# Layer 0 attention with one head in each 32-row group of TensorE, and three elementwise passes of every tile on GpSimd

## The reference

```python
x = x + _L0_xattn_ref(_layernorm(x), ctx_2048, ...)
# in it: mask = normalised x, n = 16, e = 64, t = 256, H = 8 heads of d = 8
x = jnp.transpose(mask, (0, 2, 1))
qkv = x @ w_in.T + b_in
scores = jnp.einsum('bqhd,bkhd->bhqk', q, k) / jnp.sqrt(d)
scores = jnp.where(abs(i - j) <= 64, scores, neg)
attn = jax.nn.softmax(scores, axis=-1)
o = jnp.einsum('bhqk,bkhd->bqhd', attn, v).reshape(n, t, e) @ w_out.T + b_out
y = jax.nn.relu(jnp.transpose(o, (0, 2, 1))) * encodings      # the gate product
out = jnp.einsum('nit,io->not', y, w_ct) + b_ct[None, :, None]
```

## Time and profile before

| | us |
|---|---|
| median of 3 runs (361.88 to 362.2) | 361.92 |
| the profiled execution: its own time | 362.1 |
| its span | 360.4 |
| PE busy | 320.2 |
| DVE busy | 256.2 |
| ACT busy | 208.1 |
| GpSimd busy | 192.7 |

### The profile page before, as it was taken

How to read it: one execution, slowest core, us unless ns; L and a number is a source line. 1 busy time by engine, 2 the same in 40 slices (tenths; PEclk the granted TensorE clock), 3 DMA queues, 4 the chain that set the end, 5 groups by cost and what they waited for, 6 DMA issues and landing times.

```text
span 360.4 us, 7398 instructions
## 1 busy us (share of the span) xinstructions
PE 320.2 (89%) x2258; PEld 252.3 (70%) x2258; DVE 256.2 (71%) x935; ACT 208.1 (58%) x438; POOL 192.7 (53%) x287
## 2 busy tenths in 40 slices
PE   0689999779798898999999999899999999999993
PEld 0467768567576666767777777777777767888892
DVE  5899999999989899988323615576478846661364
ACT  2639888759687695967841341467577865213210
POOL 4757988758767585856602431515152543244733
PEclk9859999999999999999999999999999999999997
DMA  7996000000000000000000000000000000000011
GB/s 220 363 373 227 1 3 3 1 2 3 1 2 0 3 3 1 3 2 2 2 2 0 0 2 0 1 2 0 2 3 0 2 0 3 0 31 15 1 38 37
DMA packets 10150, 12.16 MB, mean 34 GB/s; under 512 B 1920, under 2 KB 8832, under 8 KB 10112
## 3 DMA queue, kind: packets, MB, share of 16 engines
q1 hardware_dynamic: 9536, 11.36, 9.2%
q10 hardware_dynamic: 576, 0.33, 0.4%
HBM read 10.64 MB, written 1.05 MB: 32 GB/s over the span
## 4 chain that ended last, share of the span: by engine, by line
PE 58%; DVE 27%; issue 8%; ACT 3%; POOL 2%; DMA 1%; POOLq 0%; DVEq 0%; SPq 0%; ACTq 0%
DVE masked L1110 10%; PE S L666 6%; PE S L339 5%; PE O L377 4%; PE ST L690 4%; PE S L472 4%; PE ST L361 4%; PE S L608 2%; PE S L536 2%; PE PJ L449 2%; PE PJ L579 2%; PE O L623 2%; PE PJ L310 2%; DVE st L1072 2%; PE XB L597 2%
## 5 line engine op out<-in xcount | busy, mean ns | idle before, releaser
L1110 DVE CUSTOM_DVE_ANT_0 masked<-S,band 128x192 bf16<-128x192 f32 x256 | 79.1, 353 | 8.4 <-PE S L339 7.3
L785 ACT ACTIVATE ex<-ST 128x384 f32<-128x384 f32 x128 | 62.2, 489 | 14.0 <-PE ST L361 13.4
L339 PE MATMUL S<-qk 128*128 128x384 f32 x128 | 53.5, 424 | 10.2 <-DVE mw L1110 8.1
L948 POOL TENSOR_SCALAR rstd<-mv 128x1 f32<-128x1 f32 x40 | 11.8, 294 | 94.2 <-DVE mv L1074 94.0
L960 POOL TENSOR_TENSOR qk<-kp,kmask 128x1024 fp32r<-128x1024 f32 x24 | 46.3, 1934 | 5.0 <-DVE kp L1208 4.9
L361 PE MATMUL ST<-qk 128*128 128x192 f32 x256 | 48.7, 273 | 0.0
L361 PEld LDWEIGHTS ST<-qk 128*128 128x128 f32 x256 | 44.5, 189 | 1.9 <-issue 1.2
L339 PEld LDWEIGHTS S<-qk 128*128 128x128 f32 x128 | 24.8, 195 | 23.3 <-issue 16.1
L1254 DVE TENSOR_REDUCE mw<-S 128x8 f32<-128x512 f32 x32 | 22.0, 687 | 17.9 <-PE S L536 17.8
L751 ACT ACTIVATE hs<-PJ,sb,cols 128x512 fp32r<-128x512 f32 x29 | 22.5, 777 | 20.6 <-PE PJ L311 20.1
L377 PE MATMUL O<-ex,v 128*32 128x192 f32 x512 | 34.2, 338 | 0.0
(11 more groups left out here) (178 smaller groups left out, 757.9 us busy)
## 6 DMA issues: line engine op xcount, KB each, us to landing
w<-in_w SPq DMA_DIRECT2D x2, 1024.0 KB, 10.1
cx<-in_cx SPq DMA_DIRECT2D x1, 1024.0 KB, 7.9
cxT<-in_cxT SPq DMA_DIRECT2D x1, 1024.0 KB, 9.6
up<-in_up SPq DMA_DIRECT2D x1, 1024.0 KB, 10.9
down<-in_down SPq DMA_DIRECT2D x1, 1024.0 KB, 11.8
out<-x SPq DMA_DIRECT2D x8, 128.0 KB, 1.7
x<-in_x SPq DMA_DIRECT2D x1, 768.0 KB, 5.6
vecs<-in_vecs SPq DMA_DIRECT2D x1, 640.0 KB, 8.0
```

Of the source, the lines that this page charges most:

```text
L339: mm(out, r32(qp[:, t % 2, g, b, P * c:P * c + P]), r32(mv_), start=True, stop=True).then_inc(s["pe_s"], 1)
L785: A(ex[:, (n // 2) % 4, 2 * w:2 * w + 2, :], ST[n % 2][:, 0:2 * WIN].rearrange("p (h k) -> p h k", h=2), ACT.Exp, scale=SCALE).then_inc(s[ ...
L1110: last = V.tensor_tensor_reduce(out=masked[:, n % 2, h, :], in0=S[n % 2][:, WIN * h:WIN * h + WIN], in1=band[:, c, :], scale=1.0, scalar=N ...
```

## The change

A head of a group now has its own 32 rows (`rows(j)`), in the order given by a permuted `w0` (`w0p`, copied by GpSimd), `b0` and `colp`. A unit is one head with both query halves. A score product has 32 rows and 192 columns: two for the scores and two for the transposed scores, all four in one row group; before it was one of 128 rows by 384 columns and two of 128 rows by 192. The masked keys `kb` and all that builds them (GpSimd L960, ACT L761) are gone. The negated maxima come from a GpSimd scale of 128x16 (`neg`), and PE adds them to the queries in `MT` (one product of 512 columns and four of 128) in place of four transposes; ACT copies 128 rows of `MT` instead of 32.

The gate product and both normalisations move from DVE to GpSimd (except tile 0's `xn`). `ST_LAG` goes from 11 to 13, and what follows it moves by one or two slots. GpSimd does the selects of four units in a row instead of two. Loads on the ACT queue grow from 4 to 11: `b0` in four parts and `colp` in four. `mw` and the memset of it move behind the units.

```diff
-ST_LAG, PV_LAG = 11, 16
+NEG_LAG, MT_LAG, ST_LAG, PV_LAG, O_LAG = 9, 10, 13, (16, 18), 26
@@ PE, slot_
-                    mv_ = kb[:, t % 2, g, 2 * w:2 * w + 2, b, BAND * c:BAND * c + WIN]
-                    out = S[n % 2][:, 0:2 * WIN].rearrange("p (h k) -> p h k", h=2)
-                    mm(out, r32(qp[:, t % 2, g, b, P * c:P * c + P]), r32(mv_), start=True, stop=True).then_inc(s["pe_s"], 1)
+                    for c in range(2):
+                        last = mm(S[n % 2][:, WIN * c:WIN * c + WIN], r32(qp[rows(j), t % 2, g, b, P * c:P * c + P]),
+                                  r32(kp[rows(j), t % 3, g, b, BAND * c:BAND * c + WIN]), start=True, stop=True)
+                    last.then_inc(s["pe_s"], 1)
-                    for h in range(2):
-                        last = mm(ST[n % 2][:, WIN * h:WIN * h + WIN], r32(kb[:, t % 2, g, 2 * w + h, b, P * c:P * c + P]),
-                                  r32(qp[:, t % 2, g, b, BAND * c:BAND * c + WIN]), start=True, stop=True)
+                    for c in range(2):
+                        last = mm(ST[n % 2][:, WIN * c:WIN * c + WIN], r32(kp[rows(j), t % 3, g, b, P * c:P * c + P]),
+                                  r32(qm[rows(j), t % 2, g, b, BAND * c:BAND * c + WIN]), start=True, stop=True)
+                    pe.wait_ge(s["pool_neg"], k + 1)
+                    mm(MT[:, :].rearrange("p (g q) -> p g q", g=2), r32(identr[:, :]), r32(qp[:, t % 2, :, b, :]), start=True, stop=False)
+                            last = mm(MT[:, T * g + P * c:T * g + P * c + P], r32(neg[:, b, 2 * c + g, :]), r32(identr[:, :]),
+                                      start=False, stop=(g, c) == (1, 1))
@@ ACT
-            load(b0[:, :], a["b0"], "ld_w0")
+            for j in range(4):
+                load(b0[rows(j), :], a["b0"].rearrange("(r j d) n -> j r d n", r=4, j=4)[j], "ld_b0")
+                load(colp[rows(j), :], a["cols"].rearrange("(r j d) n -> j r d n", r=4, j=4)[j][:, :, 0:2], "ld_b0")
-                        last = A(r32(kb[:, t % 2, 1, j, 1, :]), kp[:, 1, 1, :], ACT.Copy, scale=kmask[:, j:j + 1])
+                    A(r32(qm[:, t % 2, :, b, :]), MT[:, :].rearrange("p (g q) -> p g q", g=2), ACT.Copy).then_inc(s["act_mt"], 1)
@@ GpSimd
-                G.tensor_tensor(r32(kb[:, t % 2, g, :, b, :]), kp[:, g, b:b + 1, :].to_broadcast([P, 4, T]),
-                                kmask[:, :, None].to_broadcast([P, 4, T]), ALU.mult).then_inc(s["pool_kb"], 1)
+            G.tensor_copy(w0p, w0[:, :, :].rearrange("p n (r j d) -> p n j r d", r=4, j=4)).then_inc(s["pool_w0"], 1)
+            def normalise(dst, t, name):
+                G.tensor_scalar(dst, x[:, t, :], mv[:, t, 0:1], rstd[:, t:t + 1], ALU.subtract, ALU.mult).then_inc(s[name], 1)
+                if l == 4 and 1 <= t < TILES:
+                    normalise(xn[:, t % 2, :], t, "pool_xn")
+                if l == 8 and 0 <= t < TILES:
+                    pool.wait_ge(s["act_relu"], t + 1)
+                    G.tensor_tensor(yr[:, 1, :], yr[:, 0, :], cx[:, t, :], ALU.mult).then_inc(s["pool_y"], 1)
+                if l == 14 and 0 <= t < TILES:
+                    pool.wait_ge(s["f_rstd"], t + 1)
+                    normalise(x_norm(t), t, "pool_fxn")
@@ DVE
-            dve.wait_ge(s["ld_w0"], 32)
+            dve.wait_ge(s["ld_b0"], 16 * 8)
+            dve.wait_ge(s["pool_w0"], 1)
-                        V.tensor_tensor(yr[:, 1, :], yr[:, 0, :], cx[:, t, :], ALU.mult).then_inc(s["dve_y"], 1)
-                        V.tensor_scalar(x_norm(t), x[:, t, :], mv[:, t, 0:1], rstd[:, t:t + 1], ALU.subtract, ALU.mult).then_inc(s["f_xn"], 1)
-                        normalise(xn[:, t % 2, :], t, "dve_xn")
```

More of the change, by code:

```diff
@@ L164, in parts, with rows, normalised @@
         def parts(r):
-            return r // 8, (r % 8) // 4, (r % 4) // 2, r % 2
+            return r // 8, (r % 8) // 4, r % 4
+        def rows(j):
+            return slice(32 * j, 32 * j + 32)
+        def normalised(t):
+            return (s["dve_xn"], 1) if t == 0 else (s["pool_xn"], t)
         def xg(t, k):
@@ L363, in slot_ @@
                     last.then_inc(s["pe_st"], 1)
[L366 to L380, removed]
@@ new lines, in slot_ @@
+                for c in range(2):
+                    t, r = place(T_, l, PV_LAG[c])
+                    if r % 4 == 3 and live(t, r):
+                        b, g, _ = parts(r)
+                        q = (UNITS * t + r) // 4
+                        pe.wait_ge(s["pool_sel"], 2 * q + c + 1)
+                        pe.wait_ge(s["act_v"], t + 1)
+                        if (g, c) == (0, 0) and q >= 2:
+                            pe.wait_ge(s["act_o"], q // 2)
+                        for j in range(4):
+                            last = mm(O[rows(j), T * g + BAND * c:T * g + BAND * c + WIN],
+                                      v0[:, t % 2, c, b, 4 * g + j, :], ex[:, q % 3, j, c, :],
+                                      start=(c == 0), stop=(c == 1), skip_group_check=True)
+                        last.then_inc(s["pe_pv"], 1)
@@ L383, in slot_ @@
+                t, r = place(T_, l, O_LAG + 2)
+                if r % 8 == 0 and live(t, r):
                     k = 2 * t + r // 8
@@ L750, in slot_ @@
                             act.wait_ge(s["dve_mix"], m - 1)
-                        A(r32(hs[:, m % 2, :]), proj_bank(t, n)[:, :], ACT.Identity, bias=sb0[:, n:n + 1], scale=cols[:, n // 2:n // 2 + 1])\
+                        A(r32(hs[:, m % 2, :]), proj_bank(t, n)[:, :], ACT.Identity, bias=sb0[:, n:n + 1], scale=colp[:, n // 2:n // 2 + 1])\
                             .then_inc(s["act_hs"], 1)
[L753 to L760, removed]
-                        last = A(r32(kb[:, t % 2, 1, j, 1, :]), kp[:, 1, 1, :], ACT.Copy, scale=kmask[:, j:j + 1])
-                        if j == 3:
-                            last.then_inc(s["act_kb"], 1)
                 if l == 0 and 0 <= T_ < TILES:
@@ L987, in slot_ @@
[L987 to L989 removed]
+                if l == 14 and 0 <= t < TILES:
+                    pool.wait_ge(s["f_rstd"], t + 1)
+                    if t == 0:
+                        pool.wait_ge(s["dve_spread"], 1)
+                    normalise(x_norm(t), t, "pool_fxn")
+                t, r = place(T_, l, NEG_LAG)
+                if r % 8 == 0 and live(t, r):
+                    b = r // 8
+                    k = 2 * t + b
+                    pool.wait_ge(s["dve_max"], 8 * k + 8)
+                    if k >= 2:
+                        pool.wait_ge(s["pe_mt"], k - 1)
+                    else:
+                        pool.wait_ge(s["pool_zero"], 3)
+                    G.tensor_scalar(r32(neg[:, b, :, :].rearrange("p a (j f) -> p a j f", f=32)[:, :, :, 24]), top[:, b, :, :], -1.0, None, ALU.mult)\
+                        .then_inc(s["pool_neg"], 1)
```

245 lines of the change are left out of this document (115 added, 130 removed).

## The result

The changed kernel takes 452.76 us (median of 4 runs, 452.53 to 452.82) where the kernel before takes 362.06 (4 runs, 361.88 to 362.44): a ratio of 1.2502, 95% interval 1.2481 to 1.2524. The forecast of 348 us, its range and its sign are wrong.

What follows compares the result with a forecast made beforehand. It took DVE as the bound, 19.92 of 21.16 us a tile. Start +2.6, tile 0 -1.0, tile 1 -1.2, tiles 2 to 6 -15.8, tile 7 -0.6, tail +2.2: -13.8 from 362.1, predicted 348 us, range 343.5 to 360.

Steps and rivals of the forecast that it cites:

- Clock 1.00 after tile 0: Expected sign in the changed kernel: TensorE's granted clock stands at 1.00, its 2.4 GHz level, once tile 0 is over.
- The clock falls: Rival, chance 0.06: 32-row products keep less of the array at work; at 1.2 GHz TensorE needs up to 31 us a tile.
- TensorE's need, 15.5 us: TensorE's time per steady tile after the change: 16.3 - 2.6 (scores) + 1.4 (shape changes) + 0.4 (maxima in `MT`).
- The overlap: Score products in two row groups run at once: 0.24 us a unit instead of 0.40, 2.6 us less a tile.
- a change of 0.10: Price of one change of shape on TensorE, 0.10 us; 14 more a tile, 1.4 us.
- the 16.3 that it starts from: TensorE's estimated need per steady tile before the change: 14.2 us for sixteen units plus 2.0 for projections and values.
- the allowance of 1.7: Time per steady tile added to DVE's 16.3 us because TensorE is close to it, giving 18.0 us a tile.
- DVE's need, 16.3: DVE's time per steady tile, falling from 19.92 to 16.3 us.
- The stretch, 2.08 us: Three DVE instructions lengthened beside GpSimd's key multiplies return to 0.42, 0.35 and 0.42 us, saving 2.08 us a tile.
- Late GpSimd: Rival, chance 0.13: GpSimd's normalisation or gate product comes 0.8 us a tile late and DVE waits; 352 us.
- The start, +2.6: Before the first maximum: weights' cast waits for nine ACT-queue loads at 0.47 us an issue, +3.7, less 1.1; net +2.6 us.

Runs made afterwards that it cites:

- the run with burst and added work: Changed kernel plus 24 products of 128x512 ahead of tile 1's first unit, and from tile 1 two 128x512 products ahead of each projection: 437.18 us.
- the run with 128 rows: Changed kernel with each score product over all 128 rows instead of 32, so its output sums four heads: 369.31 us.

## Why the prediction was wrong

**The step that failed** is "Clock 1.00 after tile 0", with 0.06 given to "The clock falls". All of TensorE's terms were priced at the 2.4 GHz level of the earlier trace rows, and the change takes away what keeps that level. The rival had the mechanism and the price: "up to 31 us a tile" and "over 410"; measured 31.49 and 452.76. What I should have weighed: the earlier trace rows gives 0.68 in the stretch where little but scores and projections run, with TensorE busy 12.73 of 16.03 us, so the level was not secure, and all the score products, 0.40 of a unit's 0.89 us, went from 128 rows to 32. That the rows count is shown: the clock does not rise by itself at 32 rows, is up at times at 64 and nearly always at 128, with the same changes of shape at 32 and 64. Without overlap it stays at 0.50, after a burst it falls back, and with the passes on DVE nothing changes: these three are not the cause. Changes of shape alone are not enough either (1.00 from 77 us with 32 more a tile), but they delayed the rise, so that they do a part of it together with the rows is not excluded.

The Trainium skill (TensorE: Matmul & The Clock Gate, Part 1) says that activity releases the throttle and speaks of how busy TensorE has been. Here TensorE is busy for 154.44 of 156.26 us at a clock of 0.50, so a busy engine is not enough: the rows in use count. The same page (Part 3) prices row groups at their speed-up alone; here they overlap as it says, and the lost clock costs more.

**TensorE's need, 15.5 us:** too low, which the clock hides. Half of 31.49 is 15.7, but not everything halves: four score products and L388's eight take 0.69 and 0.80 us of the chain at 1.2 GHz, 0.39 and 0.46 at 2.4, so the estimate from 31.49 is 18.0. From tile 5 of the run with burst and added work it is 18.7 (21.53, less 1.12 in which TensorE is idle and 1.7 for the eight products). The overlap is not what was mis-sized: two such groups in a row take 0.61 us there (168.39 to 169.00), as 2 x 0.24 and a change of 0.10 would. Which term is short is open; the 16.3 that it starts from is a candidate. Against 18.0 to 18.7 the 19.8 of that tile leave 1.1 to 1.8, so the allowance of 1.7 was fair. **DVE's need, 16.3:** 16.8 in the run with 128 rows and 16.94 in that tile 5. **The stretch, 2.08 us:** L1167 and L1180 as forecast; L1197 at 0.587 instead of 0.42, as the selects that stretch it stayed. **The overlap:** right, 0.01 us apart. **Late GpSimd:** not seen in the changed kernel, where everything waits for TensorE; its normalisation, taken as at most 0.74, takes 1.235.

**The start, +2.6:** measured +5.3. An issue of these small loads takes 0.64 us (the first 1.23), not 0.47, so the last of the nine begins at 6.5, not 4.5, and it lands after 5.2 us, not 4.6; the cast starts at 11.73, not 9.1. With two loads the first maximum comes 6.0 us earlier.

Even with the clock up the change would hardly win: five tiles at the estimated 19.8 save 6.8 us against 21.16, and the start takes 5.3 of them back. The run with 128 rows shows the same: 5.7 us won in its tiles, more lost at both ends.

**Open:** how much work of the whole array, and how placed, would hold the upper level (eight 128x512 products a tile, after a burst, do it at times, one 128x256 a unit does not); whether the changes of shape have a share in it; and what one change of shape costs at 2.4 GHz.

## What to carry to other kernels

A change that puts TensorE's products on fewer rows can cost the engine half its clock, even if it is never idle and even if the rows saved only multiplied by zeros; ask first what share of the products would still use all 128 rows, and read the granted clock of the changed kernel before any other row. When an instruction on DVE is two or three times as long as its shortest instance, look for what GpSimd does in that moment: moving three multiplies by one to four slots gave 1% here, but see what it hits in its new place. Price small strided loads by an issue of their own kind.

## What the runs showed of the hardware

- The granted clock follows the rows in use: the kernel before, in which most rows of a head's keys are zero, holds 1.00; the scores made on the 32 rows that count hold 0.50 for 246 us.
- After a burst of the whole array the upper level lasted 3.2 us into the row-group products.
- Two products in different row groups start 0.01 us apart; this gave 3.8 us a tile at 1.2 GHz. Four score products in two groups take 0.69 us of the chain at 1.2 GHz and 0.39 at 2.4.
- An elementwise DVE instruction can be held until the one beside it on GpSimd is nearly done: the selection, 0.35 us alone, ran from 99.50 to 101.32 with a multiply from 99.34 to 101.24.
- GpSimd takes 1.235 us for a 128x256 subtract and multiply with two per-row scalars, and 0.722 for a product of two tensors of that size.
- The clock record can lack its first part, and the mean clock then reads 0.999 for a kernel at half clock; the length of a whole-array product (415 ns in runs at 0.50, 274 to 282 in the kernel before at 1.00, for 128x256) tells the level.
